# Turning the experts' second product round, and giving half of the conversions to POOL

## What is computed

```python
mask = one_hot(top_k(x @ Wg + bg, 2)).sum(-2)            # two of the 8 experts per row
h = gelu(einsum('td,edh->teh', xf, W1) + b1)             # 64 -> 128 hidden values, every expert
y = einsum('teh,ehd->ted', h, W2) + b2                   # 128 -> 64, the second product
out = einsum('ted,te->td', y, mask)                      # the two chosen experts, added to the rows
```

## Time and profile before

| | us |
|---|---|
| median of 3 runs | 359.78 |
| runs | 358.92, 359.78, 363.84 |
| span of the profiled execution (first to last instruction) | 359.7 |
| the same, against the median of the runs | 0.1 below it |
| PE busy in the span | 264.0 (73%) |
| DVE busy | 213.2 (59%) |
| ACT busy | 152.4 (42%) |
| POOL busy | 72.6 (20%) |

### The profile page before, as it was taken

How to read it: one execution, slowest core, us unless ns; L and a number is a source line. 1 busy time by engine, 2 the same in 40 slices (tenths; PEclk the granted TensorE clock), 3 DMA queues, 4 the chain that set the end, 5 groups by cost and what they waited for, 6 DMA issues and landing times.

```text
span 359.7 us, 5155 instructions
## 1 busy us (share of the span) xinstructions
PE 264.0 (73%) x1958; PEld 193.5 (54%) x1958; DVE 213.2 (59%) x477; ACT 152.4 (42%) x271; POOL 72.6 (20%) x199
## 2 busy tenths in 40 slices
PE   2936028269799989978762598896797579999991
PEld 1834013135587878745541466693677236667671
DVE  0487329463546372364458536747638869997991
ACT  1234000002222364244452643336611898789970
POOL 9916000000223230000088000003000021233200
PEclk9996555556999999995895667689567679999996
DMA  9066616320000000000000000000000000000001
GB/s 195 37 202 120 154 42 118 99 92 2 0 13 2 1 3 0 2 1 0 2 0 0 0 0 3 1 0 0 2 0 2 0 0 13 8 17 18 16 15 26
DMA packets 11324, 10.83 MB, mean 30 GB/s; under 512 B 8728, under 2 KB 10264, under 8 KB 10776
## 3 DMA queue, kind: packets, MB, share of 16 engines
q1 hardware_dynamic: 10868, 8.76, 10.3%
q10 hardware_dynamic: 432, 1.76, 1.5%
HBM read 7.89 MB, written 2.62 MB: 29 GB/s over the span
## 4 chain that ended last, share of the span: by engine, by line
PE 49%; DVE 22%; ACT 11%; DMA 10%; issue 3%; SPq 2%; POOL 1%; DVEq 0%; ACTq 0%; POOLq 0%
PE psum L1331 8%; DMA scr_qk<-arena 4%; DMA arena<-scr_qk 4%; ACT early L557 4%; PE psum L1591 4%; DVE arena L1075 3%; PE psum L1379 3%; PE psum L1318 2%; PE psum L1467 2%; PE psum L1501 2%; DVE mneg L740 2%; PE psum L1383 2%; PE psum L1334 2%; PE psum L1222 2%; PE psum L1447 2%
## 5 line engine op out<-in xcount | busy, mean ns | idle before, releaser
L557 ACT ACTIVATE early<-psum,pk_att,scale 128x450 f32<-128x450 f32 x64 | 41.9, 733 | 5.5 <-PE psum L1576 5.4
L1276 PE MATMUL psum<-arena 128*128 128x130 bf16 x128 | 19.6, 290 | 30.7 <-DMA arena<-scr_qk 24.3
L1075 DVE SCALAR_TENSOR_TENSOR arena<-early,scale,arena 128x900 f16<-128x900 f32 x32 | 35.5, 1153 | 6.6 <-POOL arena L381 4.9
L740 DVE TENSOR_REDUCE mneg<-psum 128x3 f32<-128x390 f32 (+1 forms) x48 | 23.2, 516 | 25.2 <-PE psum L1276 23.9
L343 POOL COPY arena<-arena 128x8 f32<-128x8 f32 x128 | 18.4, 202 | 96.3 <-PE psum L1334 85.8
L762 DVE RECIPROCAL rden<-psum 64x130 f32<-64x130 f32 x16 | 15.5, 968 | 30.7 <-PE psum L1334 30.7
L1331 PE MATMUL psum<-arena 128*128 128x130 f32 x256 | 32.0, 277 | 0.0
L1575 PE MATMUL psum<-arena,amp 128*128 128x450 f16 x64 | 25.3, 396 | 9.0 <-ACT early L557 6.3
L1276 PEld LDWEIGHTS psum<-arena 128*128 128x128 bf16 x128 | 9.8, 118 | 39.7 <-issue 17.3
L381 POOL TENSOR_SCALAR arena<-early,scale 128x900 f16<-128x900 f32 x6 | 16.4, 2730 | 70.8 <-ACT early L557 70.8
L1331 PEld LDWEIGHTS psum<-arena 128*128 128x128 f32 x256 | 30.2, 191 | 0.2
(11 more groups left out here) (257 smaller groups left out, 567.1 us busy)
## 6 DMA issues: line engine op xcount, KB each, us to landing
scr_qk<-arena SPq DMA_DIRECT2D x8, 195.0 KB, 3.7
arena<-scr_qk SPq DMA_DIRECT2D x8, 195.0 KB
pk_enc<-pack_enc_dram SPq DMA_DIRECT2D x1, 1061.0 KB, 7.2
arena<-scr_qk SPq DMA_DIRECT2D x8, 130.0 KB
arena<-x_dram SPq DMA_DIRECT2D x4, 256.0 KB, 5.2
pk_ffn<-pack_ffn_dram ACTq DMA_DIRECT2D x1, 768.0 KB, 5.3
pk_qkv<-pack_qkv_dram SPq DMA_DIRECT2D x1, 690.0 KB, 5.9
pk_att<-pack_att_dram ACTq DMA_DIRECT2D x1, 626.0 KB, 3.8
```

The source lines that it names most:

```text
L557: nc.scalar.activation(hid[:, t % 2, e, :], bank[up_bank(t, e)][:, 0:2 * LOUT], ACT.Gelu, bias=col["eb1"][:, e:e + 1], scale=inv_up).then_ ...
L740: nc.vector.tensor_reduce(mneg[:, h, cols], bank[units[0] % 2][:, 0:n * TOK].rearrange("p (a n) -> p a n", a=n), AX_X, ALU.max, negate=Tru ...
L1075: nc.vector.scalar_tensor_tensor(hparts[:, t % 2, 1, two, :], hid[:, t % 2, two, :], s_hid, hparts[:, t % 2, 0, two, :], ALU.mult, ALU.sub ...
L1276: last = mm(bank[units[0] % 2][:, TOK * a:TOK * a + TOK], QS[h][:, u, s, g, TOK * j:TOK * j + P], KS[h][:, s, g, TOK * j:TOK * j + TOK], s ...
```

## The change

The second product is turned round. `down_tile` now keeps the weights stationary and moves 450 rows: per expert one matmul with both parts of the weights (128 columns stationary) on the first parts, and one with the weights' first part (64 columns stationary) on the second parts, which lands on the upper or the lower 64 partitions by the expert's parity. With one matmul for the bias that is 17 per tile. The result, `y`, has features on partitions. `output_rows`, a new DVE step, copies it to `yT` in SBUF (128 x 450, float32). `out_tile`, a new PE step, turns it back with four float32 matmuls, `yT` stationary (113 columns) and `ident2` (two identities of 64 stacked) moving; this also adds the two halves. `output_tile` is then one DVE instruction of 113 x 256. `osb` has its axes in another order, and `ob` is gone.

In tiles 1 to 6 POOL makes the first parts of groups 0 and 2, DVE of group 1, ACT of group 3. DVE's `hidden(t)` is cut in two: `hidden_first` (groups 1 and 0) and `hidden_last` (groups 3 and 2), with `output_rows(t-1)` between them from tile 3 on. PE's list becomes `down_tile(0)`, `gates(1)`, `out_tile(0)`, `up_tile(2)`, `down_tile(1)`, `mask_rows(1)`, `out_tile(1)`, `up_tile(3)`, `down_tile(2)`, then `up_tile(t)`, `out_tile(t-2)`, `down_tile(t-1)`, and at the end `out_tile(6)`, `down_tile(7)`, `out_tile(7)`. `ident2` adds 64 columns to the 640 of the first pack that is loaded.

```diff
     def down_bank(t):
-        return 5 if t > HALF and t % 2 else 3
+        return 5 if t >= HALF - 1 and t % 2 else 3
+
+    def out_bank(t):
+        return 6 + t % 2 if t >= HALF - 2 else 3
...
             for t in range(1, PAIRS - 1):
-                pool.wait_ge(S["gelu_done"], E_N * t + 4)
...
+                for n, g in enumerate((0, 2)):
+                    pool.wait_ge(S["gelu_done"], E_N * t + 2 * g + 2)
...
-                    if e == 6:
+                    if e == 6 and t in (0, PAIRS - 1):
                         first_part(t, 2)
...
+            def output_rows(t):
+                dve.wait_ge(S["down_done"], t + 1)
+                nc.vector.tensor_copy(yT[:, t % 2, :], bank[down_bank(t)][:, 0:2 * LOUT]).then_inc(S["yt_ready"], 1)
+
             def output_tile(t):
-                dve.wait_ge(S["down_done"], t + 1)
+                dve.wait_ge(S["y_done"], t + 1)
                 if t >= 2:
                     dve.wait_ge(S[f"out_stored{t % 2}"], 32 * (t // 2))
...
-            hidden(1)
-            output_tile(0)
+            hidden_first(1)
+            hidden_last(1)
+            output_rows(0)
             norm2_transposed(1)
             choose(1)
-            hidden(2)
-            output_tile(1)
+            output_tile(0)
+            hidden_first(2)
+            hidden_last(2)
+            output_rows(1)
             for t in range(HALF, PAIRS):
                 mask_row(t)
+            output_tile(1)
             for t in range(3, PAIRS):
-                hidden(t)
-                output_tile(t - 1)
+                hidden_first(t)
+                output_rows(t - 1)
+                hidden_last(t)
+                if t > 3:
+                    output_tile(t - 2)
+            output_tile(PAIRS - 2)
+            output_rows(PAIRS - 1)
             output_tile(PAIRS - 1)
...
             def down_tile(t):
...
+                if t < HALF - 1:
+                    if t:
+                        pe.wait_ge(S["o_ready"], t)
+                else:
+                    pe.wait_ge(S["mk_ready"], PAIRS)
+                    pe.wait_ge(S["yt_ready"], t - 1)
+                    pe.wait_ge(S["o_ready"], min(t - 1, HALF - 2))
+                y = bank[down_bank(t)]
+                for n, g in enumerate((0, 1, 2, 3) if t in (0, PAIRS - 1) else (1, 0, 3, 2)):
+                    pe.wait_ge(S["lo_ready"], GROUPS * t + n + 1)
+                    for e in (2 * g, 2 * g + 1):
+                        mm(y[:, 0:2 * LOUT], down2[:, e, :, :].rearrange("p k d -> p (k d)"), hparts[:, t % 2, 0, e, :],
+                           start=n == 0 and e % 2 == 0, stop=False)
+                    for e in (2 * g, 2 * g + 1):
+                        r = D * (e % 2)
+                        mm(y[r:r + D, 0:2 * LOUT], down2[:, e, 0, :], hparts[:, t % 2, 1, e, :], start=False,
+                           stop=n == GROUPS - 1 and e % 2 == 1)
+                mm(y[0:D, 0:2 * LOUT], b2r[:, :], xb[:, 2 * t:2 * t + 2, :].rearrange("p b n -> p (b n)"),
+                   start=False, stop=True).then_inc(S["down_done"], 1)
+
+            def out_tile(t):
+                pe.wait_ge(S["yt_ready"], t + 1)
+                if t >= HALF - 2:
+                    pe.wait_ge(S["mk_ready"], PAIRS)
+                    pe.wait_ge(S["o_ready"], t - 1)
+                for ch in range(2):
+                    for bb in range(2):
+                        a, n = LOUT * bb + STEP * ch, D * (2 * ch + bb)
+                        last = mm(bank[out_bank(t)][0:CH, n:n + D], yT[:, t % 2, a:a + CH], ident2, start=True, stop=True)
+                last.then_inc(S["y_done"], 1)
```

More of the change, by code:

```diff
@@ L48 @@
 GROUPS = 4
-ARENA = 27440
+ARENA = 27840
 Q_TERM = (0, 0, 0, 1, 1, 2)
@@ L57 @@
 PACKS = {
-    "dft": [("dft", 2 * L), ("ident", P)],
+    "dft": [("dft", 2 * L), ("ident", P), ("ident2", D)],
     "qkv": [("posenc", TOK), ("wq", P), ("wk", P), ("wv", P), ("wv_stack", D), ("bq", 1), ("bk", 1),
@@ L102, in audio_tower @@
         dft = col["dft"].rearrange("p (c n) -> p c n", c=2)
-        ident = col["ident"]
+        ident, ident2 = col["ident"], col["ident2"]
         vl_mask = col["vl_mask"].rearrange("p (s d) -> p s d", s=2)
@@ L1077, in second_part, with hidden_first, hidden_last @@
                                                ALU.subtract).then_inc(S["lo_ready"], 1)
-            def hidden(t):
+            def hidden_first(t):
                 if t >= 2:
                     dve.wait_ge(S["down_done"], t - 1)
-                alone = t in (0, PAIRS - 1)
                 made_before = t + (t > 0)
-                first_part(t, 0)
-                dve.wait_ge(S["hi_dve"], made_before + 1)
-                second_part(t, 0)
-                if alone:
-                    first_part(t, 1)
-                    dve.wait_ge(S["hi_dve"], made_before + 2)
-                else:
-                    dve.wait_ge(S["hi_pool"], t)
-                second_part(t, 1)
-                for g in (2, 3):
-                    dve.wait_ge(S["hi_act"], 2 * t + g - 1)
-                    second_part(t, g)
+                if t in (0, PAIRS - 1):
+                    for g in (0, 1):
+                        first_part(t, g)
+                        dve.wait_ge(S["hi_dve"], made_before + g + 1)
+                        second_part(t, g)
+                else:
+                    first_part(t, 1)
+                    dve.wait_ge(S["hi_dve"], made_before + 1)
+                    second_part(t, 1)
+                    dve.wait_ge(S["hi_pool"], 2 * t - 1)
+                    second_part(t, 0)
+            def hidden_last(t):
+                acts_before = t + (t > 0)
+                if t in (0, PAIRS - 1):
+                    for g in (2, 3):
+                        dve.wait_ge(S["hi_act"], acts_before + g - 1)
+                        second_part(t, g)
+                else:
+                    dve.wait_ge(S["hi_act"], acts_before + 1)
+                    second_part(t, 3)
+                    dve.wait_ge(S["hi_pool"], 2 * t)
+                    second_part(t, 2)
             for b in range(2 * HALF):
@@ L1578, in down_tile @@
             def down_tile(t):
-                if t:
-                    pe.wait_ge(S["o_ready"], t if t <= HALF else t - 1)
-                parts = [(bb, ch) for bb in range(2) for ch in range(2)]
-                for e in range(E_N):
-                    if e % 2 == 0:
-                        pe.wait_ge(S["lo_ready"], GROUPS * t + e // 2 + 1)
-                    for bb, ch in parts:
-                        o = bank[down_bank(t)][0:CH, 2 * D * (2 * bb + ch):2 * D * (2 * bb + ch) + 2 * D]
-                        a = LOUT * bb + STEP * ch
-                        mm(o, hparts[:, t % 2, 0, e, a:a + CH], down2[:, e, :, :].rearrange("p k d -> p (k d)"),
-                           start=e == 0 and (bb, ch) == (0, 0), stop=False)
-                        mm(o[:, 0:D], hparts[:, t % 2, 1, e, a:a + CH], down2[:, e, 0, :], start=False, stop=False)
@@ L1594, in down_tile @@
-                for bb, ch in parts:
-                    n = 2 * D * (2 * bb + ch)
-                    last = mm(bank[down_bank(t)][0:CH, n:n + D], xb[:, 2 * t + bb, STEP * ch:STEP * ch + CH], b2r[:, :],
-                              start=False, stop=(bb, ch) == (1, 1))
-                last.then_inc(S["down_done"], 1)
+                if t < HALF - 1:
+                    if t:
+                        pe.wait_ge(S["o_ready"], t)
+                else:
+                    pe.wait_ge(S["mk_ready"], PAIRS)
+                    pe.wait_ge(S["yt_ready"], t - 1)
+                    pe.wait_ge(S["o_ready"], min(t - 1, HALF - 2))
@@ L1704, in _ @@
             gates(1)
+            out_tile(0)
             up_tile(2)
@@ L1707, in _ @@
             mask_rows(1)
+            out_tile(1)
             up_tile(3)
@@ L1711, in _ @@
                 up_tile(t)
+                out_tile(t - 2)
                 down_tile(t - 1)
+            out_tile(PAIRS - 2)
             down_tile(PAIRS - 1)
+            out_tile(PAIRS - 1)
 def host_packs(w):
@@ L1738, in host_packs @@
     c["ident"] = np.eye(P, dtype=f)
+    c["ident2"] = np.concatenate([np.eye(D, dtype=f)] * 2)
     pos = np.arange(TOK)[:, None].astype(np.float64)
```

31 lines of the change are left out of this document (15 added, 16 removed).

## The result

The change made the kernel slower: median 369.95 us (368.73 to 371.43) against 360.25 (358.92 to 363.84), ratio 1.0252 with a 95% interval of 1.0187 to 1.0318, so slower by 1.9 to 3.2%. The forecast was 369.0, in a range of 365.8 to 372.3.

What follows compares the result with a forecast made beforehand. DVE sets the pace to about 322 us, then PE's steps with gelu's pace inside up_tile, and slow stores at the end. Later PE steps and serial stores bring the end to 368.9, first load 0.1: predicted 369.0, range 365.8 to 372.3.

Steps and rivals of the forecast that it cites:

- Order in PE's list: Head: up_tile(3) waits behind out_tile(1) for DVE, starting 4.1 us late; up_tile(4) 3.7 late; the largest part.
- Turning back: Each out_tile: eight float32 instructions at 0.11 us, 0.9 with handover; bounds 0.44 and 1.10.
- the shorter product: Each down_tile: 17 matmuls at 0.191 us take 3.25 instead of 3.67, saving 0.42 per tile.
- a cheap turning: Rival for out_tile 1 to 5: 0.44 us each, saving 2.2, so 366.8; chance 0.07.
- no shorter product: Rival for down_tile 2 to 6: a tile keeps 3.67 us, adding 2.1, so 371.1; chance 0.05.
- ACT's relief: One conversion less in tiles 1 to 6, counted as nothing; rival: 2.5 us less, 366.5, chance 0.10.
- DVE and POOL: Conversions and second parts per tile: nothing added; rival: they lock each other out, 15 us more, 384, chance 0.03.
- the signs of being wrong: Trace signs: up_tile(3) before 311, up phase near 3.1, 450-column matmuls 0.375 apart behind a pause, second parts beyond 1.2.
- The first load: Start: ident2 is a tenth of a 320 KB load, adding 0 to 0.4 us; 0.1 taken.
- The half clock: Rival at waits before down_tile(1) and out_tile(1): one down_tile at twice its price, 3.1 us more, 372.1; chance 0.10.
- The end: Output 7 waits for tile 5's store, landing 4.85 us later; three streams in a row end at 368.1, span 368.9.
- The forecast of 2.8 for the stores: End of span: PE's side alone would have ended at 366.1 instead of 368.9, so stores cost 2.8 us.

Runs made afterwards that it cites:

- after_head: Changed kernel with tiles 0 and 1 turned back into own banks, down_tile waiting only for DVE's copy, out_tile(1) behind down_tile(2); ratio to kernel before 1.0231.
- after_order: Changed kernel with output_tile(0) ahead of choose(1) and out_tile(1) inside up_tile(3), behind its fourth expert; ratio to kernel before 1.0180.
- after_slots: Changed kernel with four osb slots instead of two, so output 7 waits for no store; ratio to kernel before 1.0284.
- after_stores: Changed kernel with each 113-row store issued as 112 rows and one row; ratio to kernel before 1.0124.

## Why the prediction was right, step by step

**Order in PE's list: right.** `up_tile(3)` was forecast 4.1 late and came 3.8 late, `up_tile(4)` 3.7 and 3.5. The copy was released a little earlier, and eight float32 matmuls with the handover took 0.84 rather than 0.95. That it is the waits in the list and not the work is shown by after_head, which gets 2.8 back by moving `out_tile(1)` behind two steps and freeing `down_tile(1)` of its wait for an output. That second wait the prediction had seen, and rightly priced at nothing while the longer one stood behind it. What I had not seen is that a place half-way is no better: after_order waited 2.38 for the same copy and lost the clock on top.

**Turning back and the shorter product: right sum, two sizes off.** The turning took 0.75, not 0.9: 0.094 per instruction, below the 0.11 that I took and nearer to it than to 0.055. The product took 3.38, not 3.25, so the saving is 0.29, not 0.42. One price for both widths was wrong in kind, as one group of four shows in PE's timeline (the first line is the second matmul of its pair):

```profile
324.40 0.35 PE L1616 MATMUL psum<-arena,pk_dft 128*128 128x450 f16 x1
324.69 0.38 PE L1620 MATMUL psum<-arena,pk_dft 128*64 128x450 f16 x2
```

The two matmuls with 64 stationary columns, which write the lower and the upper 64 partitions, both start at 324.69, and the two together take 0.38: they run side by side. (The last pair is followed by the bias matmul, 64 wide too, 0.21 later.) But from 128 columns to 64 the starts are 0.29 apart, and from 64 back to 128 (the next group starts at 325.00) 0.31, where two of 128 are 0.19 to 0.20 apart. So what running side by side saves is lost at the two changes of width, and a group takes 0.80, a little over 4 x 0.19. That the price of 0.191 came near is luck; what fewer changes of width would bring was not tried.

The tile came to 7.82 against 7.83 only because the errors cancel. The rivals of a cheap turning and of no shorter product both lose, but each by less than I had thought.

**ACT's relief: right that it is worth nothing.** The swap of the shares moved no steady tile in either kernel. The rival falls.

**DVE and POOL: right in the sum, wrong in kind.** I had no second part above 1.156 and added nothing, and put a stretch beyond 1.2 among the signs of being wrong. The longest was 1.907, and two of the 32 were that long, 1.5 us in all; from tile 4 on PE's steps show no wait for it. POOL's pair took 6.63, over the 5.1 to 6.5 that I had, so its slack was 0.7 (done 8.8 us into the tile, needed at 9.5) and not 1. By the Trainium skill (SBUF — State Buffer, "SBUF: two separate sides") the engine that starts first holds the shared port pair for its whole instruction and the other blocks. The trace bears this out for POOL, whose conversions grow by what is left of DVE's second part, and not for DVE: the two parts that began 0.23 behind a conversion of 2.71 took 0.75 longer, and no wait of about 2.5 showed.

**The first load: too small to see.** It grew from 320 to 352 KB and landed in 3.6 us, against 3.7.

**The half clock: right for this kernel.** The waits before `down_tile(1)` and `out_tile(1)` were 1.12 and 1.45, within the "1 to 1.5" of the prediction, and the clock stayed. Behind a longer one, 2.38, after_order was granted 0.57, with a tile's product at 4.18 instead of 3.38.

**The end: right, and 1.0 too short.** That output 7 would wait for tile 5's store and that three streams follow each other was right: after_slots and after_stores show both. From the end of output 5 (354.30) to the end of the last stream, about 366.8, it took 12.5; I had 11.5. Tile 5's store landed 5.56 after its output (354.69 + 5.17 on the chain), not the 4.85 of the earlier trace rows, and the two streams behind it took 7.0, not 6.65; what lengthened them was not tried. This, with an output 5 that came 0.4 earlier, makes up the 0.6 by which the forecast from `up_tile(0)` (368.9 - 279.13 = 89.8) was short of 90.36. The forecast of 2.8 for the stores and the 2.63 measured are close by luck, as they are not the same thing: the 2.8 is against a last store that is just as slow but waits for nothing, the 2.63 is what the change loses to the stores beyond what before does. By the forecast's reckoning, with output 7 of after_slots and 4.85 + 0.8 behind it, the measured queue is 90.36 - 86.79 = 3.6; the same in before is 80.57 - 79.62 = 0.95, and the difference of the two is the 2.6.

**The time of a launch.** I set the sum against the span, as the listing of before had nothing else. In after the launch of the profiled run is 369.51 and its span 367.6; the part before the experts was 1.9 shorter here than in the profile of before. The two 1.9 cancel by chance, so the last microsecond of the agreement is luck.

## What to carry to other kernels

Before a step is put into a queue, ask what its own wait is for and what stands behind it: moved past two steps that didn't need it, and with a second wait taken out, the same work cost 0.7 us instead of 3.5. A shorter product that needs a further step pays only if that step finds idle time on the engine that sets the pace, and taking load from an engine that waits paid nothing in the steady tile. Look at the last stores first: dividing 113 rows into 112 and 1 was worth more than any other single edit tried here, though each further store is a further half microsecond on SP's list, which shows when two outputs come close.

## What the runs showed of the hardware

- A store of 113 rows (56.5 KB) runs as one stream at 18 GB/s. Issued as 112 + 1 rows in every tile, it takes 3.66 us off the end of one kernel and 6.29 off that of the other. An issue takes SP about 0.5 (six in 3.03).
- A conversion on POOL (2.53 alone) that begins while a second part of DVE runs takes about 2.4 and what is left of that part. A second part that begins 0.23 behind a conversion takes 1.91 instead of 1.15, one that begins 1.5 or more behind it 1.15.
- Two matmuls of 450 moving columns with 64 stationary columns each, on the lower and the upper 64 partitions of the result, start together. From 128 stationary columns to 64 and back the starts are 0.29 and 0.31 apart instead of 0.19, so that four matmuls in this order take 0.80.
- PE at 2.4 GHz kept its clock behind a pause of 1.45, and was granted mostly 1.2 GHz behind one of 2.38.
